# A recommender tower on one core: lows signalled in pieces, paced gathers, and transposes moved one place earlier

## What is computed

```
e = jnp.stack([tbl_0[ids[:, 0]], ..., tbl_26[ids[:, 26]]], axis=1)
z = einsum('bnd,bmd->bnm', e, e)[lower triangle]          # 351 pairs of a row
h = concatenate([z, dense_ctx], axis=1)                   # 367 columns
h = maximum(h @ W_top1 + b_top1, 0.0)                     # 512
h = maximum(h @ W_top2 + b_top2, 0.0)                     # 256
y = h @ W_top3                                            # 1
```

## Time and profile before

| | |
|---|---|
| median of 3 runs | 106.79 us (106.44 to 106.99) |
| profiled execution, whole / its span | 106.66 us / 104.8 us |
| TensorE matmul busy | 99.6 us, 95% |
| VectorE busy | 79.5 us, 76% |
| ScalarE busy | 71.5 us, 68% |
| GpSimd busy (60 gathers) | 62.1 us, 59% |
| TensorE clock granted | 1.00 throughout |

### The profile page before, as it was taken

How to read it: one execution, slowest core, us unless ns; L and a number is a source line. 1 busy time by engine, 2 the same in 40 slices (tenths; PEclk the granted TensorE clock), 3 DMA queues, 4 the chain that set the end, 5 groups by cost and what they waited for, 6 DMA issues and landing times.

```text
span 104.8 us, 2680 instructions
## 1 busy us (share of the span) xinstructions
PE 99.6 (95%) x1012; PEld 86.4 (82%) x1012; DVE 79.5 (76%) x240; ACT 71.5 (68%) x151; POOL 62.1 (59%) x68
## 2 busy tenths in 40 slices
PE   5989997999999999999999998999999988999992
PEld 5858785888888888888887797999999978999980
DVE  5599999999999899998969949996259540952212
ACT  4486999599896999969796359893358431961240
POOL 3777777777887777777777777777777300000000
DMA  2887998978849767589922222322222200000000
GB/s 54 237 195 221 195 222 177 229 184 189 199 102 245 176 167 170 117 236 327 353 74 53 55 58 53 85 68 59 73 53 59 68 6 0 6 12 12 6 1 0
DMA packets 5541, 12.57 MB, mean 120 GB/s; under 512 B 2066, under 2 KB 2804, under 8 KB 5401
## 3 DMA queue, kind: packets, MB, share of 16 engines
q1 hardware_dynamic: 3585, 8.44, 30.2%
q0 software_dynamic: 1920, 3.94, 16.0%
q10 hardware_dynamic: 24, 0.02, 0.1%
HBM read 12.15 MB, written 0.00 MB: 116 GB/s over the span
## 4 chain that ended last, share of the span: by engine, by line
PE 77%; DVE 7%; DMA 5%; ACT 4%; issue 2%; SPq 2%; DVEq 0%
PE acc L408 19%; PE acc L400 17%; PE gram_ps L438 12%; PE acc L456 11%; PE tr_ps L372 6%; PE acc L476 5%; DMA table<-in_tbl 5%; PE gram_ps L456 3%; DVE onehot L579 3%; DVE pairs L532 2%; PE gram_ps L381 2%; PE tr_ps L476 2%; DVE lo L585 2%; ACT embT L636 1%; SPq L295 1%
## 5 line engine op out<-in xcount | busy, mean ns | idle before, releaser
L358 POOL DMA_INDIRECT emb<-in_tbl,ids_sb x60 | 61.3, 1021 | 19.4 <-issue 18.0
L579 DVE TENSOR_SCALAR onehot<-idrel 125x512 fp32r<-125x512 f32 x90 | 32.1, 425 | 1.8 <-ACT idrel L650 1.8
L400 PE MATMUL acc<-onehot,hi 125*128 125x512 f32 x102 | 26.3, 400 | 0.2 <-DVE onehot L579 0.2
L408 PE MATMUL acc<-onehot,lo 125*128 125x512 f32 x102 | 25.7, 393 | 0.8 <-DVE lo L585 0.8
L408 PEld LDWEIGHTS acc<-onehot,lo 125*128 125x128 f32 x102 | 18.8, 188 | 5.9 <-DVE lo L585 2.1
L400 PEld LDWEIGHTS acc<-onehot,hi 125*128 125x128 f32 x102 | 18.6, 188 | 4.1 <-issue 0.3
L532 DVE COPY pairs<-gram_ps 26x96 f32<-26x96 f32 (+1 forms) x64 | 16.5, 258 | 7.1 <-PE gram_ps L438 5.8
L532 ACT COPY pairs<-gram_ps 26x96 f32<-26x96 f32 (+1 forms) x64 | 15.2, 238 | 7.5 <-PE gram_ps L438 6.1
L585 DVE TENSOR_TENSOR lo<-table,hi 125x256 fp32r<-125x256 f32 x51 | 18.1, 412 | 0.0
L636 ACT COPY embT<-acc 128x512 f32<-128x512 f32 (+2 forms) x13 | 13.4, 1048 | 6.8 <-PE acc L408 6.7
L438 PEld LDWEIGHTS gram_ps<-embT 128*58 128x58 f32 x512 | 14.2, 133 | 2.3 <-issue 1.8
(11 more groups left out here) (48 smaller groups left out, 56.2 us busy)
## 6 DMA issues: line engine op xcount, KB each, us to landing
table<-in_tbl SPq DMA_DIRECT2D x8, 480.0 KB
table<-in_tbl SPq DMA_DIRECT2D x3, 600.0 KB
w_sb<-in_W SPq DMA_DIRECT2D x1, 1024.0 KB, 8.2
emb<-in_tbl,ids_sb POOLq DMA_INDIRECT x60
w_sb<-in_W SPq DMA_DIRECT2D x1, 512.0 KB, 9.4
table<-in_tbl SPq DMA_DIRECT2D x2, 240.0 KB
pairs<-pairs SPq DMA_DIRECT2D x16, 15.0 KB
table<-in_tbl SPq DMA_DIRECT2D x8, 20.0 KB
```

What stands on the lines that cost most here:

```text
L358: pool.indirect_dma_start(emb[:, t % EMB_RING, gathered_features.index(f), :], None, tables[f], bass.IndirectOffsetOnAxis(ids_sb[:, t, f:f ...
L400: return nc.tensor.matmul(acc[:, b, 0:batch], hi[0:ROWS_K, b, c, :], one_hot(k, c), start=(c == 0), stop=False)
L408: return nc.tensor.matmul(acc[:, b, 0:batch], lo[0:ROWS_K, b, c, :], one_hot(k, c), start=False, stop=(c == CHS[k] - 1))
L579: nc.vector.tensor_scalar(one_hot(k, one), idrel[0:ROWS_K, b, 0:batch], float(one), None, ALU.is_equal).then_inc(onehot_by_dve, 1)
```

## The change

Four edits. (1) `lo_ready` is raised by every subtraction, one for two chunks, and `low(c)` waits at every even chunk for the piece that it needs; `pieces_to(k)` counts pieces in place of `parts_to(k)`, in the reload wait too, which keeps its meaning. (2) Transposes tr(2,0), tr(2,1), tr(2,2) and tr(3,3) each move one place ahead in `STEPS`. (3) For gathers of the first three tiles, n = 8, 10, ... 44, GpSimd first waits until VectorE has made min(23n//10 - 13, 90) one-hots. (4) The last tile's four groups wait for the end of the lookups, for both grams of tile 0, for both of tile 1, and for h1(0).

```diff
-        STEPS = tr(1, [3]) + [("gram", 0, 0), ("gram", 0, 1)] + tr(2, [0]) + [("gram", 1, 0)] + tr(2, [1]) + [("gram", 1, 1)]
-        STEPS += tr(2, [2]) + [("h1", 0, None)] + tr(2, [3]) + [("h2", 0, None), ("gram", 2, 0)] + tr(3, [0]) + [("gram", 2, 1)]
-        STEPS += [("h1", 1, None)] + tr(3, [1, 2]) + [("h2", 1, None)] + tr(3, [3])
+        STEPS = tr(1, [3]) + tr(2, [0]) + [("gram", 0, 0), ("gram", 0, 1)] + tr(2, [1]) + [("gram", 1, 0)] + tr(2, [2])
+        STEPS += [("gram", 1, 1), ("h1", 0, None)] + tr(2, [3]) + [("h2", 0, None), ("gram", 2, 0)] + tr(3, [0])
+        STEPS += [("gram", 2, 1), ("h1", 1, None)] + tr(3, [1, 2, 3]) + [("h2", 1, None)]
...
+        def pieces_to(k):
+
+            return sum(CHS[:k]) // 2
...
-                    sp.wait_ge(lo_ready, parts_to(k - RING + 1))
+                    sp.wait_ge(lo_ready, pieces_to(k - RING + 1))
...
+                    if t == LAST:
+
+                        pool.wait_ge(*[(looked_up, NK), (gram_done, UNITS), (gram_done, 2 * UNITS), (h1_done, H1C)][g])
                     for f in group(t, g):
+                        n = t * len(gathered_features) + gathered_features.index(f)
+                        if n >= 8 and n % 2 == 0 and t < LAST:
+
+                            pool.wait_ge(onehot_by_dve, min(23 * n // 10 - 13, sum(DVE_CHS)))
...
                 def low(c):
 
-                    for n, part in enumerate(parts(k)):
-                        if c == part.start:
-                            pe.wait_ge(lo_ready, parts_to(k) + n + 1)
+                    if c % 2 == 0:
+
+                        pe.wait_ge(lo_ready, pieces_to(k) + c // 2 + 1)
...
-                        last = nc.vector.tensor_tensor(lo[0:ROWS_K, b, two, :], table[0:ROWS_K, r, two, :],
-                                                       hi[0:ROWS_K, b, two, :], ALU.subtract)
-                    last.then_inc(lo_ready, 1)
+                        nc.vector.tensor_tensor(lo[0:ROWS_K, b, two, :], table[0:ROWS_K, r, two, :],
+                                                hi[0:ROWS_K, b, two, :], ALU.subtract).then_inc(lo_ready, 1)
```

## The result

| | before | changed |
|---|---|---|
| median | 106.60 us (20 runs) | 106.16 us (20 runs) |
| ratio | | 0.9942, 95% interval 0.9918 to 0.9965 |
| span of the profiled execution | 104.8 | 104.3 |

The change is worth 0.6% by the ratio and 0.44 us by the medians, where 105.7 was forecast for 106.79; the middle of the forecast gain was 1.1 us.

A forecast was written before the change was run, and what follows sets the result against it. TensorE, busy 95%, was taken as the bound; 1.55 us won at the lookups, 1.35 left at h1(0) and 1.1 at gram(3,0) after waits, gave 105.7 against 106.79. Range 105.0 to 106.5.

The forecast's parts named there:

- The lows in pieces: Lookups: TensorE's lows start on first subtractions; 1.30 us at k = 2 plus 0.25 at the last table, 1.55 together.
- Does the third table let 0.32 through? ... It just does: Third table: ninth one-hot ready at 15.85, TensorE wants it at 15.9, so the 0.32 us gained earlier passes.
- The moved transposes: Tower: transposes fill the wait before gram(0,0), which starts 1.30 us earlier; h1(0) and what follows 1.35 earlier.
- the 0.3 us left before gram(1,0): Gram(1,0) waits for VectorE to empty the PSUM buffer it shares with gram(0,0); 0.35 us of standing stays.
- the wait of h1(0) for moved rows: h1(0) wants the moved rows at 67.55, they are seen at 68.0; a wait of 0.45 us charged.
- The last transposes: tr(3,3) ahead of h2(1) runs at 83.67, held by the last gather; gram(3,0) at 85.79, 1.1 us earlier.
- The estimate of 0.4 from last bytes to semaphore: Last gather before tr(3,3): its signal shows 0.4 us after its last bytes move, judged from tile 0's row moves.
- The Trainium skill's estimate of 2.15 us: Landing time of a 64 KB gather: 83.5 counted from its row's start, 84.5 from its end; not used in the sum.
- The waits on GpSimd: Gathers: new waits never bind; 23 of them cost at most 0.2 us at 0.01 each, nothing charged.
- The sum: Whole kernel: 1.1 us gain, 105.55 for the profiled execution, 105.7 against 106.79.
- the rival of late signals: Row moves of tile 0 or last gather show late: gain 0 to 0.5 us, 106.3 to 106.8; chance 0.19.
- 0.60, 0.15 and a third of 0.19: Chances added for faster: own forecast (gain 0.8 to 1.5), gather not holding tr(3,3) (gain 1.7), part of late signals.

The follow-up runs named there:

- edit 1 alone: Kernel before, with only the lows waiting for pieces and an increment on each subtraction; 105.64 us against 106.78, ratio 0.9889.
- edit 1 and tr(3,3): Kernel before plus lows in pieces and only tr(3,3) moved ahead of h2(1), no GpSimd waits; 106.17 us against 106.67, ratio 0.9953.
- two gathers fewer: Changed kernel with gathers n = 13 and 14 of tile 0 replaced by plain SyncE transfers of 128 rows; 106.56 us against 106.67, ratio 0.9962.
- the second group: Four variants of the changed kernel's transpose order on a chip with a lower TensorE clock; 137.56 to 139.44 us, kernel before 155.25; questions unanswered.
- third group: Here the kernel before with lows in pieces and only tr(3,3) moved ahead of h2(1), no GpSimd waits; 106.17 us against 106.67.

## Why the prediction was right, and where not

**The lows in pieces: right, and the size in part by luck.** 1.30 at L385 and 1.55 at the end of the lookups were forecast; edit 1 alone shows 1.19 (19.99 to 18.80) and 1.45 (59.22 to 57.77). But the stop that it removes is not the same in each execution: the lows of k = 2 waited 0.68 us in the profile that the sum was read from, 0.45 with GpSimd's waits alone (L388 at 19.78) and 0.32 with the moved transposes alone (L381 at 19.62), and the lookups of these three are the same instructions. Against the latter two edit 1 wins 0.98 and 0.82 at L385. No one-hot held k = 3 or 4, and 51 increments in place of 14 cost VectorE nothing that the trace shows: five subtractions take 1.75 where they took 1.76.

**In the changed kernel's profile 0.9 of this was lost at once, in a step that the prediction did not have.** "Does the third table let 0.32 through? ... It just does" looked at VectorE only. Between the two tables stands tr(0,0), and it wants gathers that the trace of before could not show as late, since no reader had come early enough: there TensorE reached it at 14.02. The profiles of the kernels with edit 1, by when SyncE issued the load of the third table:

| kernel | load issued | TensorE ready for tr(0,0) | tr(0,0) starts |
|---|---|---|---|
| changed | 5.21 | 13.80 | 14.65 |
| changed, no waits of GpSimd | 5.34 | 13.81 | 13.91 |
| edit 1 and tr(3,3) | 6.03 | 13.84 | 13.84 |
| two gathers fewer | 6.21 | 13.78 | 14.08 |
| edit 1 alone | 6.50 | 13.81 | 13.81 |
| changed, tr(3,1) ahead of h1(1) | 6.56 | 13.81 | 13.81 |

The delay is not that of GpSimd's waits: these gathers, n = 0 to 3, have none, a stop is there without the waits, and the last row has them and no stop. More bytes of tables ahead of the gathers' may be a reason, as the two earliest loads have a stop; but the order of the table does not follow it throughout (6.21 has a longer stop than 5.34, though with two more transfers of SyncE at 8.27), and it was not tried. The kernel with tr(0,0) one table later, which would have told the stop's worth, is one of the second group.

**The moved transposes: the sizes right, their worth not.** Gram(0,0) behind seven transposes, the 0.3 us left before gram(1,0), and the wait of h1(0) for moved rows (0.45 charged, 0.64 measured: 68.28 + 0.23 to 69.15) came as forecast. But I booked the start of h1(0) 1.79 earlier less that wait, and did not compare with leaving tr(2,2) where it was: the moved rows are tied to gram(0,0), which stands 0.2 later by the move of tr(2,0). Where the order was left, h1(0) took them up with no wait (edit 1 and tr(3,3)) or after 0.20 (edit 1 alone), with four transposes in the time before it.

**The last transposes: the mechanism right, the holder of this profile not.** A wait at tr(3,3) in place of the 0.76 us before gram(3,0): yes. At 83.67 for the gather: 83.79 with that name where TensorE comes early (third group), but 84.17 with ScalarE's copy named in the changed kernel, because tr(3,1) was 1.16 later there than forecast (82.80, 81.64). The estimate of 0.4 from last bytes to semaphore was good: in the third group's kernel the last bytes move between 83.2 and 83.4 and the gather shows at 83.75. The Trainium skill's estimate of 2.15 us for it ("DMA: Bandwidth & Descriptors", "Anatomy of one DMA — SWDGE (gpsimd) path"), counted from the start of GpSimd's row, is 0.44 below the 2.59 of the chain.

**The waits on GpSimd: right,** 0.01 us each at most, and neither gain nor loss alone that can be told. **The sum:** the term that was mis-sized is the first one as it arrives in this kernel, 0.58 in place of 1.55 us at the end of the lookups; the middle of the forecast, 1.1 us, is more than twice the 0.44 of the medians, and the time lies in the range because the range was wide. Gram(3,0) at 86.41 lies by the 86.4 of the rival of late signals, given 0.19, but by luck: the transfers that it named were not to blame, as the row moves were seen 1.48 us after their issue where 1.30 was reckoned, and the last gather held nothing in this profile. The late signal was that of the first gathers. One slip besides: 0.60, 0.15 and a third of 0.19 are 0.81, and not 0.78.

## What to carry to other kernels

When TensorE is brought forward, walk its own order and ask of every instruction on the way that reads a transfer when that transfer really shows; a trace in which nobody waits for it gives only an upper bound. A transpose that waits for the end of a slow steady stream can be moved ahead only while TensorE comes late enough: the move of tr(3,3) gained 0.30 us where tr(3,1) started at 82.80, and cost 0.55 on balance where it started at 81.63, though it did away with 0.73 us of visible idle time before gram(3,0). Measure the parts alone, and look at the single executions and more than one profile: one of four edits showed 1.1% and all four 0.6%, but the intervals overlap, and a stop of 0.85 us was in one profile of the same instructions and not in another.

## What the runs showed of the hardware

A transfer's signal is the loosest time in the trace. Four row moves of 15 KB show at SyncE 1.30, 1.35, 1.38, 1.48, 1.67 and 1.95 us after the end of the last issue for tile 0 in six kernels, and for tile 1 either 1.4 us (with edit 1 alone, 74.50 less 73.11, and in the changed kernel) or 2.8 to 3.0 (before, 77.72 less 74.75, and in the three others). The Trainium skill's rule that an increment lands only after every earlier write of its DMA engine, across queues ("DMA: Bandwidth & Descriptors", section "Queues, rings and completion order", the passage on HWDGE ordering), could be behind the late ones, but the trace of before does not settle it: by the bytes moved in stretches of 0.1 us the fourth move is through by 76.1, an estimate, and a gather's bytes run behind it from 76.6 to 77.1, so the rule fits only if these count as earlier. It was not tested. GpSimd starts a gather of 64 KB every 1.25 us alone and every 1.35 beside the lookups, and its signal comes 2.59 us from its start in a quiet place, and up to 7.5 us beside the first table loads.
